# Turning the attention probabilities on VectorE and by DMA instead of on TensorE

## What is computed

```
bq = q.reshape(b, h, nw, w, d)              # 16 heads of 64, windows of w = 32 tokens
bk2, bv2 = (look(bk), look(bv))             # each window and the one before it: 64 keys
sim = jnp.einsum('bhwie,bhwje->bhwij', bq, bk2) * QK_SCALE
sim = jnp.where(mask, -jnp.finfo(sim.dtype).max, sim)
attn = jax.nn.softmax(sim, -1)
out = jnp.einsum('bhwij,bhwje->bhwie', attn, bv2)
```

## Time and profile before

| | |
|---|---|
| median of 3 runs | 1962.6 us (1961.4 to 1962.93) |
| the profiled execution: its own time | 1961.85 us |
| the profiled execution: span of the trace | 1960.1 us |
| busy share of the span | PE 92%, PE weight loads 64%, DVE 76%, ACT 63%, POOL 63% |
| chain that ended last | PE 49%, DVE 14%, issue 8%, POOL 6%, ACT 6% |

### The profile page before, as it was taken

The page is one execution under the profiler, slowest core; times in us unless marked ns, Lnnn a source line. Parts: engine busy times, 40 slices in busy tenths (PEclk is TensorE's granted clock), DMA queues, the critical chain, the costliest instruction groups (busy, mean ns, idle before and its releaser), DMA issues.

```text
span 1960.1 us, 75595 instructions
## 1 busy us (share of the span) xinstructions
PE 1809.8 (92%) x31926; PEld 1253.5 (64%) x31926; DVE 1488.0 (76%) x2822; ACT 1241.2 (63%) x2413; POOL 1234.4 (63%) x789
## 2 busy tenths in 40 slices
PE   7477876999999999999999999999999999999995
PEld 2144453667667667777777767677767776666773
DVE  6699947878777778787878777787878787777763
ACT  6523214577676767676767676767676767677662
POOL 3466733766666666666666666666666666666650
PEclk9799967999999999999999999999999999999996
DMA  4444002222222242222423222422224222222220
GB/s 100 123 53 56 17 3 83 63 67 67 67 66 62 68 117 71 64 72 60 122 70 73 63 67 61 125 61 72 62 70 121 70 64 69 65 67 67 66 69 22
DMA packets 89777, 137.48 MB, mean 70 GB/s; under 512 B 27168, under 2 KB 32736, under 8 KB 88416
## 3 DMA queue, kind: packets, MB, share of 16 engines
q1 hardware_dynamic: 89440, 132.66, 28.2%
HBM read 29.79 MB, written 2.10 MB: 16 GB/s over the span
## 4 chain that ended last, share of the span: by engine, by line
PE 49%; DVE 14%; issue 8%; POOL 6%; ACT 6%; DVEq 0%; SPq 0%; ACTq 0%; POOLq 0%; DMA 0%
PE bank L1435 8%; PE bank L1342 8%; PE bank L1417 7%; PE bank L1355 7%; PE bank L1390 5%; DVE turnedhalf L1762 5%; PE bank L1347 5%; PE bank L1452 4%; PE bank L1476 3%; POOL probs L1304 3%; DVE qk L1758 2%; POOL qk L1280 2%; DVE rnorm L1768 2%; ACT q_T L1604 1%; DVE probs L1781 1%
## 5 line engine op out<-in xcount | busy, mean ns | idle before, releaser
L1286 POOL TENSOR_TENSOR qk<-qk,rnorm 128x1024 f32<-128x1024 f32 x192 | 361.4, 1903 | 366.0 <-ACT rnorm L1592 275.4
L1280 POOL TENSOR_TENSOR qk<-qk,turnedhalf 128x1024 f32<-128x1024 f32 x192 | 454.7, 2368 | 138.8 <-DVE turnedhalf L1762 138.8
L1758 DVE TENSOR_TENSOR qk<-bank,gains 128x512 f32<-128x512 f32 x384 | 262.8, 684 | 222.0 <-ACT squares L1582 207.8
L1342 PE MATMUL bank<-wqkv,x 128*128 128x512 f32 x768 | 378.1, 596 | 4.7 <-DVE v_tok L1738 2.9
L1582 ACT ACTIVATE squares<-bank 128x512 f32<-128x512 f32 x384 | 232.6, 606 | 153.4 <-PE bank L1342 150.6
L1762 DVE TENSOR_TENSOR turnedhalf<-bank,gains 128x256 f32<-128x256 f32 x768 | 286.3, 414 | 0.0
L1629 ACT ACTIVATE o_T<-bank 128x512 f32<-128x512 f32 x192 | 104.2, 598 | 229.5 <-PE bank L1417 229.5
L1768 DVE TENSOR_REDUCE rnorm<-squares 128x16 f32<-128x1024 f32 x192 | 230.8, 1202 | 2.8
L1417 PEld LDWEIGHTS bank<-p_T,v_win 64*64 64x64 f32 x12288 | 189.9, 135 | 60.2 <-issue 57.6
L1355 PEld LDWEIGHTS bank<-st_ident,qk 128*128 128x128 f32 x1536 | 178.6, 142 | 57.1 <-issue 50.9
L1347 PE MATMUL bank<-wqkv,x 128*128 128x512 f32 x384 | 202.5, 609 | 7.0 <-DVE turnedhalf L1762 6.9
(11 more groups left out here) (197 smaller groups left out, 2946.9 us busy)
## 6 DMA issues: line engine op xcount, KB each, us to landing
v_win<-v_tok SPq DMA_DIRECT2D x1536, 64.0 KB
wqkv<-in_wqkv SPq DMA_DIRECT2D x6, 1536.0 KB
v_rep_sb<-v_by_step SPq DMA_DIRECT2D x32, 128.0 KB
v_rep<-v_by_step SPq DMA_DIRECT2D x32, 128.0 KB
wo<-in_wo SPq DMA_DIRECT2D x6, 512.0 KB
w<-in_w SPq DMA_DIRECT2D x6, 341.0 KB
w<-in_w SPq DMA_DIRECT2D x6, 192.0 KB
xT_sb<-in_xT SPq DMA_DIRECT2D x1, 1024.0 KB, 4.9
```

What stands on the lines that cost most here:

```text
L1280: nc.gpsimd.tensor_tensor(out=qk[n % 2][:, half], in0=qk[n % 2][:, half], in1=turnedhalf[:, half], op=ALU.add).then_inc(rot_added.sem, 1)
L1286: nc.gpsimd.tensor_tensor(out=by_head(qk[u][:, half]), in0=by_head(qk[u][:, half]), in1=rnorm[u][:, AH * i:AH * (i + 1)].unsqueeze(2).to_b ...
L1342: nc.tensor.matmul(QK_BANKS[i][:, :], shifted_tokens(x, n, P), layer_cols(wqkv, n, 3 * INNER, 512 * i, 512), start=True, stop=True).then_i ...
L1758: nc.vector.tensor_tensor(by_head(qk[u][:, cols]), src, cos.to_broadcast([P, 8, DH]), ALU.mult).then_inc(rotated.sem, 1)
```

## The change

PE's `turn_p` and ACT's `read_p` go. DVE gets `turn_p`: one transposing instruction, which turns each square of 32 x 32 within its 32 partitions, 128x1024 elements, into a new tile `p_blocks`. The keys of a window are then on the partitions of the window's queries, its two halves of 32 keys side by side. SP's new `place_p` brings the eight pieces (4 windows x 2 halves, 64 KB each) to their partitions in `p_T`, which has two buffers now. It waits for `p_turned`, for `outputs` of two blocks earlier and for the transfers of the block before.

The values are no longer spread by window. `p_T` has two sides: for windows 1 and 3 of a block the 64 keys are the tokens of `v_tok` as they stand; for windows 0 and 2 they are the tokens one window earlier, so `place_v` makes one copy `v_shift`, 32 tokens later, with two transfers. `v_tok` has 4 slots instead of 3. `outputs` loads the values of one head (64 keys x 64) and streams 32 columns of `p_T`, as before in shape and number, but in another order: the two loops g (which 64 partitions are contracted) and p (which 64 partitions of the bank are written) have g outside. The weights `wo` are laid out for the new order of heads on the host. The results go to the banks of k's transposes (`T_BANKS`), so `turn_k` now waits for `read_o` of two blocks earlier and `turn_q` for `shifts`.

```diff
+LAG_P = 2
-V_SLOTS = 3
+V_SLOTS = 4
...
-    v_win = two("v_win", (P, WINDOWS, INNER // 2))
-    probs, p_T = two("probs", (P, PAIRS, 2, DH)), sb("p_T", (P, PAIRS, P))
+    v_shift = two("v_shift", (P, INNER))
+    probs, p_T = two("probs", (P, PAIRS, 2, DH)), two("p_T", (P, 2, AH, WINDOW))
+    p_blocks = sb("p_blocks", (P, 2, AH, WINDOW))
...
     def sync(sp):
         def place_v(n):
...
-            for p in range(2):
-                cols = slice(p * INNER // 2, (p + 1) * INNER // 2)
-                for w in range(WINDOWS):
-                    own, before = slice(WINDOW * w, WINDOW * (w + 1)), slice(WINDOW * (w - 1), WINDOW * w)
-                    sp.dma_start(v_win[u][DH * p + WINDOW:DH * (p + 1), w, :], tok[own, cols]).then_inc(v_placed.sem, 16)
-                    src = tok[before, cols] if w else last[P - WINDOW:P, cols]
-                    sp.dma_start(v_win[u][DH * p:DH * p + WINDOW, w, :], src).then_inc(v_placed.sem, 16)
+            sp.dma_start(v_shift[u][WINDOW:P, :], tok[0:P - WINDOW, :]).then_inc(v_placed.sem, 16)
+            sp.dma_start(v_shift[u][0:WINDOW, :], last[P - WINDOW:P, :]).then_inc(v_placed.sem, 16)
+
+        def place_p(n):
+            sp.wait_ge(p_turned.sem, p_turned.after(n))
+            sp.wait_ge(o_product.sem, o_product.after(n - 2))
+            sp.wait_ge(p_placed.sem, p_placed.after(n - 1))
+            for w in range(WINDOWS):
+                for half in range(2):
+                    row = DH * (w // 2) + WINDOW * half
+                    sp.dma_start(p_T[n % 2][row:row + WINDOW, w % 2, :, :], p_blocks[WINDOW * w:WINDOW * (w + 1), half, :, :]).then_inc(p_placed.sem, 16)
+
+        def place(n):
+            if n >= LAG_P:
+                place_p(n - LAG_P)
+            place_v(n)
...
         def turn_k(n):
             pe.wait_ge(qk_made.sem, qk_made.after(n, 2))
-            transposes(T_BANKS, k_turned, qk[n % 2][:, INNER:2 * INNER], pT_made, n - 2)
+            if n == LAST:
+                transposes(k_banks(n), k_turned, qk[n % 2][:, INNER:2 * INNER], shifted, n - 1)
+            else:
+                transposes(T_BANKS, k_turned, qk[n % 2][:, INNER:2 * INNER], oT_made, n - 2)
...
-            for w in range(WINDOWS):
-                for side in range(2):
-                    for p in range(2):
-                        a_, at, rows = 2 * q + side, WINDOW * w, slice(DH * p, DH * (p + 1))
-                        mm = nc.tensor.matmul(s_banks(n)[p][DH * side:DH * (side + 1), P * q + at:P * q + at + WINDOW],
-                                              v_win[n % 2][rows, w, DH * a_:DH * (a_ + 1)], p_T[rows, a_, at:at + WINDOW],
-                                              start=True, stop=True, skip_group_check=True)
+                pe.wait_ge(p_placed.sem, p_placed.after(n))
+            for a_ in (2 * q, 2 * q + 1):
+                for turn_ in range(2):
+                    v = v_tok[n % V_SLOTS] if turn_ else v_shift[n % 2]
+                    for g in range(2):
+                        for p in range(2):
+                            rows, head = slice(DH * g, DH * (g + 1)), 2 * a_ + p
+                            at = DH * a_ + WINDOW * turn_
+                            mm = nc.tensor.matmul(o_banks(n)[g][DH * p:DH * (p + 1), at:at + WINDOW], v[rows, DH * head:DH * (head + 1)],
+                                                  p_T[n % 2][rows, turn_, head, :], start=True, stop=True, skip_group_check=True)
...
-            at(3, turn_p)
...
-            at(3, read_p)
...
+        def turn_p(n):
+            dve.wait_ge(p_normed.sem, p_normed.after(n))
+            dve.wait_ge(p_placed.sem, p_placed.after(n - 1))
+            nc.vector.transpose(p_blocks[:, :, :, :], probs[n % 2][:, :, :, :].rearrange("t a p (g k) -> t g (a p) k", k=WINDOW)).then_inc(p_turned.sem, 1)
...
         def turn(at, pair):
+            at(3, turn_p)
             pair(6, gated_full)
             at(0, rotate, 0)
```

More of the change, by code:

```diff
@@ L1246, in sync @@
             for n in range(EARLY, BLOCKS):
-                place_v(layer * BLOCKS + n)
-        for n in range(BLOCKS):
-            place_v((DEPTH - 1) * BLOCKS + n)
+                place(layer * BLOCKS + n)
+        for n in range(BLOCKS - 1):
+            place((DEPTH - 1) * BLOCKS + n)
+        place_p(LAST - 2)
+        place_p(LAST - 1)
+        place_v(LAST)
+        place_p(LAST)
         def store(n0, n1):
@@ L1616, in exponent @@
             nc.scalar.activation(pr, pr, ACT.Exp, scale=QK_SCALE).then_inc(exp_made.sem, 1)
-        def read_p(n):
-            act.wait_ge(o_product.sem, o_product.after(n - 1))
-            for i in range(2):
-                act.wait_ge(p_turned.sem, p_turned.after(n, i + 1))
-                nc.scalar.activation(p_T[:, 4 * i:4 * i + 4, :].rearrange("p a t -> p (a t)"), T_BANKS[i][:, :], ACT.Copy).then_inc(pT_made.sem, 1)
         def read_o(n):
@@ L1627, in read_o @@
             at = P * (n % PAIR)
-            for p in range(2):
-                nc.scalar.activation(o_T[:, 4 * p:4 * p + 4, at:at + P], s_banks(n)[p][:, :].rearrange("p (q t) -> p q t", t=P),
+            for g in range(2):
+                nc.scalar.activation(o_T[:, :, at + DH * g:at + DH * (g + 1)], o_banks(n)[g][:, :].rearrange("p (a t) -> p a t", t=DH),
                                      ACT.Copy).then_inc(oT_made.sem, 1)
@@ L1717, in scalar @@
         affine(m - 1)
-        read_p(LAST)
+        read_o(LAST - 1)
         read_o(LAST)
@@ L1868, in vector @@
         m = LAST_PAIR
+        turn_p(LAST - 2)
         norm_x(m - 2)
```

66 lines of the change are left out of this document (31 added, 35 removed).

## The result

The changed kernel takes 1997.88 us (median of 4 runs, 1994.75 to 1999.41), the kernel before in the same call 1962.0 us (4 runs, 1957.95 to 1962.93): a ratio of 1.0185, with a 95% interval of 1.0166 to 1.0204. The change makes the kernel 36 us slower. The profiled execution, the fastest of the four, took 1994.75 us, with a span of 1992.8 us, where the one before had 1960.1 us: 32.7 us more.

A forecast was written before the change was run, and what follows sets the result against it. PE, busy 92%, was the bound on average, with a chain through ACT, DVE and POOL only 0.3 us shorter. Pairs +26, stalls -14, load +3, end +4 gave +19 us: 1981 us, range 1940 to 2035.

The forecast's parts named there:

- Stretch 1, DVE's transpose: From the end of odd outputs to up_a_tail: transpose waits for POOL's division, delays the gate's product; +0.9 us (0.7 to 1.4).
- U: Mark in the prediction's timelines: the start of up_a_tail, the group with 128*85.
- PE's 0.93 us in the even turn gain nothing here: Between odd outputs' end and up_a_tail, the chain ACT, DVE, POOL, DVE sets the time, so dropped transposes save nothing.
- k's transposes wait 0.6 us for `read_o`: After the even turn's outputs PE waits some 0.6 us for ACT's read; covered by slack, 2 us still spare.
- Stretch 2: From up_a_tail to the end of odd outputs: project_o starts earlier, limited by add_ffn; a gain of 0.69 us (0.4 to 0.93).
- The order of `outputs`: Four records in a row on one half of the rows cost 0.4 us more per block (nothing to 2.07).
- regular pair: Two successive turns without irregular stalls: 32.47 us before, forecast +0.6 us, 33.1 us after; 44 pairs +26 us.
- Irregular stalls: Of 27 us of irregular stalls in 44 pairs, half fall into PE's new slack: -14 us (0 to -27).
- The load: Once per layer, weights queue ahead of the probabilities, which land 3.8 us late; +3 us in all (0 to 12).
- O: Mark in the prediction's timelines: the end of an odd turn's outputs.
- The end: At the last blocks, transpose and transfers are no longer hidden, so the last outputs start later: 4 us (0 to 7).
- The start: Beginning of the kernel, up to the first outputs; the prediction's sum has no term for it.

The follow-up runs named there:

- Run 7: The kernel before, plus VectorE's transpose of the divided probabilities into a tile that nobody reads; ratio 1.0126 to the kernel before.
- Run 1: The changed kernel with VectorE's transpose behind the gate's product instead of ahead of it in odd turns; ratio 1.0342 to the kernel before.
- run 5: The changed kernel with q turned ahead of k on TensorE and read in that order by ScalarE; ratio 1.0155 to the kernel before.
- run 6: The changed kernel with VectorE turning only a strip of 128x32 per block instead of 128x1024; ratio 1.0093 to the kernel before.
- run 9: The changed kernel with totals ahead of rotate 3 and GpSimd's division ahead of add_turned 1; ratio 1.006 to the kernel before.
- run 4: The changed kernel with the two inner loops of outputs exchanged, so neighbouring products contract different halves of the rows; ratio 1.0171 to the kernel before.
- run 10: As run 9, with q turned ahead of k and the third product of project_qk ahead of up_gate_full; ratio 0.9926 to the kernel before.
- run 3: The changed kernel with the next layer's weights loaded in parts over several turns, the same bytes; ratio 1.0093 to the kernel before.
- run 12: The kernel before with totals and division earlier, project_qk's third product ahead of up_gate_full, and weights loaded in parts; ratio 1.0235 to the kernel before.
- run 2: The changed kernel with the next layer's weights issued behind that turn's probabilities on SyncE's queue; ratio 1.0113 to the kernel before.

## Why the prediction was right in direction and off in size

I forecast +19 us (1981), and it became +36 by the medians and +32.7 by the profiled spans. By its own steps:

- *Stretch 1, DVE's transpose, +0.9 us.* The mechanism and the size stand: 1245 ns where I took 1.2 us, the gate's product directly behind, U 0.87 us later. Run 7 gives 0.86 us for VectorE's part alone. But one reading was wrong. The 0.94 us ahead of `up_a_tail` is idle time of the weight loader's row, PEld. PE's own row has only 0.11 us there, without a releaser:

```profile
1041.75 1.02 PE L1342 MATMUL bank<-wqkv,x 128*128 128x512 f32 x2
1042.88 0.66 PE L1452 MATMUL bank<-xn_T,w 128*85 128x256 f32 x2
```

And the gate's product, which that group waits for, had itself waited for PE. So PE's own way set the end of stretch 1. Hence "PE's 0.93 us in the even turn gain nothing here" came true for another reason as well: PE could have used them, and two waits for ACT took them. The wait for `xn_T` gave back 0.58 us (PE was 0.35 us ahead behind it instead of 0.93), the one for `o_T` behind it 0.8 us. PE's way to U so grew to 20.13 us, and the transpose only tops it by 0.42 (runs 1, 5, 6, 9).

- *k's transposes wait 0.6 us for `read_o`, covered by 2 us of slack.* The wait is there, 0.51 us. The slack wasn't. It was worked out as if PE could run 0.93 us ahead into the even `outputs`, while `up_gate_full` waits for `xn_T`, and it took PEld's 0.94 us off PE's way from there to U. That way was put at 7.05 us and is 1026.99 - 1017.88 = 9.11, of which 0.51 and 0.53 us are waits. So some 0.5 us were spare, not 2:

```profile
1017.88 0.32 PE L1445 MATMUL bank<-p_T,v_shift 64*64 64x32 f32 x8
```

- *Stretch 2, -0.69 us.* From U to `centres` it went from 12.79 to 12.26 us, -0.53. Run 1 shows its cause in reverse: work of DVE ahead of `add_ffn` delays `project_o`. From U, `project_o` starts 0.81 us earlier than before (6.43 instead of 7.24 us), and the new wait of `centres` for DVE's `xm`, 0.21 us, and the gap around it give the rest back.
- *The order of `outputs`, +0.4 us a block, +18 us.* Wrong; nothing (run 4). Without this term the forecast for a regular pair is +0.2 us, and +0.29 was measured.
- *Irregular stalls, -14 us.* -15.1 us by the commonest pairs. The half was a choice without a row behind it, so that it came so near is luck.
- *The load, +3 us.* This is the term that was mis-sized: +20 us. The probabilities were to land at O + 14.5 us, 3.8 us late, "of which 2 to 3 are spare". In the first of the loads they landed at O + 17.1 (714.65 against 697.6, the end of the odd `outputs`), and PE had waited for them since O + 11.7, no sooner than in the kernel before (11.62). So nothing was spare, for the reason just given, and it was 5.4 us late. The burst itself lasted as forecast, with the DMA engines over 80% busy until about 711.5, O + 13.9; but the probabilities landed 3 us behind it, where I had them land with it. Then came what I hadn't priced: the clock is at 0.50 behind so long a wait, and products take twice as long for some microseconds. From the start of these `outputs` to U it is 725.24 - 714.65 = 10.59 us instead of 9.11: another 1.5 us, which with the 5.4 make up the 6.9 us of this pair. In the second load the two gaps of PE's own (3.28 and 1.56 us) cost nearly as much.
- *The end, +4 us.* +8.7. The chain is the one forecast, with one link that I left out: not only the issues of the last block wait for the landing of the one before it, but its transpose too.

```profile
1935.41 1.25 DVE L1809 STREAM_TRANSPOSE p_blocks<-probs 128x1024 f32<-128x1024 f32 x1 [1.15 <-DMA p_T<-p_blocks]
...
1944.56 0.44 PE L1445 MATMUL bank<-p_T,v_shift 64*64 64x32 f32 x8 [2.38 <-DMA p_T<-p_blocks]
```

So 1.25 us of transpose come in, and the last eight issues take 6.33 us where I had put some 4.4. The last `outputs` start 36.9 us after the last regular turn instead of 29.9: 7.0 us, where I had 4. And again I priced the wait and not the clock: those last 128 records take 3.64 us instead of 2.07.

- *The start, 0.* +5.5 us in this pair of executions. Of these, 2.65 us lie ahead of the stream and aren't the change's: its first product starts at 317.49 us before and at 320.14 after, and anywhere from 315.4 to 320.4 in the 14 kernels. The other 2.85 us lie in the first `outputs`. They start as long after the first `scores` as before (20.8 and 20.7 us), although PE waits 2.9 us for `p_T`, but PE stands still in the middle of them, and this gap too ends 1.2 us behind a transfer of instructions. That the change causes it isn't shown.

```profile
367.08 0.33 PE L1445 MATMUL bank<-p_T,v_tok 64*64 64x32 f32 x4 [2.06 <-issue]
```

Of the signs that I had named, the odd turn's wait for the division, the gate's product directly behind the transpose and the lack of a wait for `p_T` in ordinary turns came. A regular pair is 32.8 us and not 33.1, `outputs` take 2.07 us and not 2.5, PE's wait ahead of `up_a_tail` is 0.53 us and not over 2, and the waits in turns with a load reach 5.4 us and not 4.

The wrong +18 us and the missing +17 and +5 partly cancel, so the forecast was nearer than its steps deserved; that is luck.

## What to carry to other kernels

Taking work off the busiest engine gains nothing until you know what it will wait for next: subtract the work, then go through each of its later instructions and look for the inputs that would now come last. Here two steps of ScalarE stood 0.5 us behind. Moving the division earlier (run 9) took the loss from 1.9% to 0.6%, and filling both waits on top of it (run 10) made a gain of 0.7%; neither was filled alone on top of run 9. A short transfer that an engine needs each turn should never queue behind a burst of weights; and an edit that is safe beside one queue order can cost 13 us at each layer beside another (runs 3 and 12).

## What the hardware showed that I had not expected

- A wait of PE costs more than its length. After 5.36 us of idle time the granted clock is 0.50, that is 1.2 of 2.4 GHz, in this window of the kernel after, though PE is busy all through it:

```profile
712.00:716.00 4.00, 1.35 (x52) 1.38 (x53) 2.40 (x3) 0.23 (x1) 3.98 (x2) 0.69 0.08 26
716.00:720.00 4.00, 4.00 (x90) 2.88 (x86) 1.25 (x1) 1.57 (x3) 0.91 (x2) 0.50 0.16 41
```

- PE's instructions come by DMA too, in pieces of 16 KB, and PE stands still when they are late: 176 of its 188 gaps without a releaser end 1.2 to 1.6 us behind such a transfer. While a load keeps the DMA engines over 90% busy, such a gap lasted 3.3 us, in `scores` of the kernel after and in `outputs` of run 2. In the turns of the kernel before the longest was 1.4 us.
- VectorE turns 128x1024 float32 in squares of 32 in 1.25 us, and one strip of 128x32 in 0.21 us.
- Four records in a row on one half of the rows are as fast as alternating halves, 2.07 us for 128 records.
